# A fused mixer and gated-experts kernel: the first block's norm alone ahead of the first product, and the work of steps 0 to 3 in another order

## The reference

```python
xn = _layernorm(x)                         # mean and variance over the 128 channels
s = _L0_attn_ref(xn, ...)                  # token mixer: 6 projections, a scan over time, group norm, output projection
# experts, R = 4 rounds, E = 4 experts, top 2:
for r in range(R):
    logits = flat @ Wg[r] + bg[r]
    vals, idx = top_k(logits, 2); w = softmax(vals)
    cw = sum(one_hot(idx, E) * w[..., None], axis=1)
    hmid = gelu(einsum('nh,ehf->enf', flat, W1) + b1)
    y = einsum('enf,efh->enh', hmid, W2) + b2
    cur = cur + einsum('ne,enh->nh', cw, y)
out = x + s * silu(cur)
```

## Time and profile before

| | us |
|---|---|
| median of 3 runs | 797.25 (796.95 to 797.36) |
| the profiled execution | 795.54 |
| its span in the trace | 793.7 |
| PE busy | 781.5 (98% of the span) |
| DVE busy | 687.8 (87%) |
| ACT busy | 642.4 (81%) |
| POOL busy | 111.9 (14%) |

### The profile page before, as it was taken

The page is one execution under the profiler, slowest core; times in us unless marked ns, Lnnn a source line. Parts: engine busy times, 40 slices in busy tenths (PEclk is TensorE's granted clock), DMA queues, the critical chain, the costliest instruction groups (busy, mean ns, idle before and its releaser), DMA issues.

```text
span 793.7 us, 9921 instructions
## 1 busy us (share of the span) xinstructions
PE 781.5 (98%) x3395; PEld 620.5 (78%) x3395; DVE 687.8 (87%) x1090; ACT 642.4 (81%) x878; POOL 111.9 (14%) x135
## 2 busy tenths in 40 slices
PE   8899999999999999999999999999999999999996
PEld 6678788887888878888788887888878887788885
DVE  7988887899888889879899788987988989998997
ACT  7989887887888878788778877887878888788884
POOL 0011111111111101111111111111111111111110
PEclk9999999999999999999999999999999999999998
DMA  8444362342534326234164322643228544365452
GB/s 263 126 88 136 60 183 62 93 102 46 125 64 106 94 40 160 58 81 103 28 146 114 76 65 40 147 107 94 44 38 172 107 75 102 63 174 123 76 121 53
DMA packets 63569, 78.46 MB, mean 99 GB/s; under 512 B 36000, under 2 KB 41632, under 8 KB 59552
## 3 DMA queue, kind: packets, MB, share of 16 engines
q0 software_dynamic: 18144, 33.04, 24.7%
q1 hardware_dynamic: 45104, 44.67, 18.7%
q10 hardware_dynamic: 272, 0.13, 0.1%
HBM read 40.34 MB, written 2.36 MB: 54 GB/s over the span
## 4 chain that ended last, share of the span: by engine, by line
PE 91%; DVE 5%; ACT 1%; issue 1%; DMA 1%; DVEq 0%; ACTq 0%
PE h_bank L985 14%; PE h_bank L981 14%; PE h_bank L982 14%; PE y_bank L1045 14%; PE y_bank L1041 14%; PE y_bank L1040 14%; PE p_bank L981 2%; PE p_bank L985 2%; PE p_bank L982 2%; PE r_bank L1080 1%; DVE g_lo L690 1%; ACT g L408 1%; DVE tmp L704 1%; ACT g_hi L414 1%; DMA cw_b<-cw_scratch 0%
## 5 line engine op out<-in xcount | busy, mean ns | idle before, releaser
L408 ACT ACTIVATE g<-h_bank,b_c 128x512 f32<-128x512 f32 x512 | 329.3, 681 | 81.2 <-PE h_bank L985 80.6
L690 DVE TENSOR_TENSOR g_lo<-g,g_hi 128x1024 fp32r<-128x1024 f32 x256 | 310.3, 1222 | 83.5 <-ACT g_hi L414 81.9
L414 ACT ACTIVATE g_hi<-g 128x1024 fp32r<-128x1024 f32 x256 | 271.8, 1062 | 8.1
L356 POOL DMA_DIRECT2D cur<-tmp x126 | 110.8, 879 | 667.8 <-DVE tmp L704 516.9
L985 PE MATMUL h_bank<-cur_lo,w_hi 128*128 128x512 f32 x512 | 204.0, 398 | 0.0
L981 PE MATMUL h_bank<-cur_hi,w_hi 128*128 128x512 f32 x512 | 203.2, 397 | 0.2 <-DVE cur_hi L601 0.2
L1040 PE MATMUL y_bank<-g_hi,w_hi 128*128 128x512 f32 x508 | 200.7, 395 | 2.3 <-DVE w_lo L580 2.1
L982 PE MATMUL h_bank<-cur_hi,w_lo 128*128 128x512 f32 x512 | 202.6, 396 | 0.0
L1041 PE MATMUL y_bank<-g_hi,w_lo 128*128 128x512 f32 x508 | 200.7, 395 | 0.0
L1045 PE MATMUL y_bank<-g_lo,w_hi 128*128 128x512 f32 x508 | 139.6, 396 | 0.0
L981 PEld LDWEIGHTS h_bank<-cur_hi,w_hi 128*128 128x128 f32 x512 | 96.4, 188 | 27.6 <-issue 4.6
(11 more groups left out here) (144 smaller groups left out, 393.9 us busy)
## 6 DMA issues: line engine op xcount, KB each, us to landing
cur<-tmp POOLq DMA_DIRECT2D x126, 256.0 KB, 3.3
cw_b<-cw_scratch SPq DMA_DIRECT2D x31, 1024.0 KB, 5.0
cur<-in_x SPq DMA_DIRECT2D x8, 256.0 KB, 5.4
xn_t<-cur SPq DMA_DIRECT2D x8, 256.0 KB, 3.4
xr<-in_x SPq DMA_DIRECT2D x28, 64.0 KB, 3.4
out<-o SPq DMA_DIRECT2D x28, 64.0 KB, 2.0
cw_b<-in_w SPq DMA_DIRECT2D x4, 256.0 KB, 3.9
cw_b<-cw_scratch SPq DMA_DIRECT2D x1, 768.0 KB, 5.4
```

The lines of the kernel that those rows point to most:

```text
L356: pool.dma_start(cur[:, block_of(s // E)], tmp[:, s % SUMS, :], accum_op=ALU.add).then_inc(summed, DMA)
L408: nc.scalar.activation(g[:, gb, ft * BLK:(ft + 1) * BLK], hb[ft][:, :], ACT.Gelu_apprx_tanh, bias=b1_c[:, e * FT + ft:e * FT + ft + 1]).th ...
L414: nc.scalar.activation(g_hi[:, gb, h], g[:, gb, h], ACT.Copy).then_inc(g_hi_done, 1)
L690: nc.vector.tensor_tensor(g_lo[:, gb, h], g[:, gb, h], as_f32(g_hi[:, gb, h]), ALU.subtract).then_inc(g_lo_done, 1)
```

## The change

Four things change, none of which alters what is computed.

1. **Block 0 alone.** `norm_first` becomes `norm_one(b)`, which makes statistics, mean and variance of one block. `norm_one(0)` and `norm_root((0,))` stand ahead of the first product, `norm_one(1)` and `norm_root((1,))` behind `low_w2(0)`. PE's chain has 11 transposes in place of 13. `turn_first` writes `p_bank` and `r_bank`, `store_first` reads them and comes later on DVE. ACT scales block 1 after `hidden(0)`, not before it, and PE turns it after `down(0)`, not before `up(1)`.
2. **The third down projection in the logits' bank.** `down(2)` writes `r_bank` and waits for `router_scores(0)` to have read the logits, not for `combine(0)`.
3. **The router of blocks 0 and 1 later.** `logits(0)` moves from behind `up(1)` to behind `up(2)`, `router_scores(0)` to the end of DVE's step 0, `router_tanh(0)` to step 1 on ACT, `router_gates(0)` to the start of DVE's step 1. `combine(0)` and `combine(1)` both stand at the end of DVE's step 1.
4. **Blocks 2 and 3.** `norm_stats((2,))` stands at the start of DVE's step 2, `norm_stats((3,))` and `norm_spread` between the two halves of `g_low_half` of step 2, and the root at the start of step 3.

The high and low parts of `w2` move too: `high_w2(2)` and `high_w2(3)` to the start of ACT's steps 1 and 2, `low_w2(2)` and `low_w2(3)` to the ends of DVE's steps 0 and 1.

The diff, cut to what moves work:

```diff
-ROOT_CHAIN = 13
+ROOT_CHAIN = 11
-NORM_GROUPS = [(0, 1), (2, 3), (4, 5, 6, 7)]
+NORM_GROUPS = [(0,), (1,), (2, 3), (4, 5, 6, 7)]
-LATE = (0, 8)
+LATE = (0, 1, 8)
+IN_R_BANK = 2
...
             high_w2(0)
-            scale_block(1)
             act.wait_ge(b1_loaded, DMA)
             hidden(0)
+            scale_block(1)
...
                 if s == 1:
                     high_w1(3)
+                    high_w2(2)
+                elif s == 2:
+                    high_w2(3)
...
                 def between():
-                    if s < E - 1:
-                        high_w2(s + 1)
+                    if s == 0:
+                        high_w2(1)
...
                 def late():
-                    if s == 0:
+                    if s == 1:
                         router_tanh(0)
...
-            norm_first()
-            norm_root((0, 1))
+            norm_one(0)
+            norm_root((0,))
...
             low_w2(0)
-            store_first()
+            norm_one(1)
+            norm_root((1,))
+            low_w1(2)
             dve.wait_ge(gate_loaded, DMA * GATEW)
             nc.vector.tensor_scalar(wg_p[:, :, 0:E], wg_c[:, :, :], 1.0, None, ALU.mult).then_inc(combined, 2)
+            g_low_half(0, 0)
+            g_low_half(0, 1)
+            store_first()
             store_second()
-            g_low_half(0, 0)
-            low_w1(2)
-            g_low_half(0, 1)
-            router_scores(0)
...
                 if s == 1:
-                    split_cur(1)
+                    router_gates(0)
                 elif s == 2:
-                    norm_root(NORM_GROUPS[1])
+                    norm_stats((2,))
                 elif s == 3:
-                    norm_stats(NORM_GROUPS[2][0:2])
+                    norm_root(NORM_GROUPS[2])
+                elif s == 4:
+                    norm_stats(NORM_GROUPS[3][0:2])
...
                     if half == 0:
-                        if s < E - 1:
-                            low_w2(s + 1)
                         if s == 0:
-                            router_gates(0)
-                        elif s == 1:
-                            dve.wait_ge(small_loaded, DMA * SMALL)
-                            combine(0)
+                            low_w2(1)
+                        elif s == 2:
+                            norm_stats((3,))
+                            norm_spread(NORM_GROUPS[2])
...
                 if s == 0:
                     low_w1(3)
+                    low_w2(2)
+                    router_scores(0)
                 elif s == 1:
-                    norm_stats(NORM_GROUPS[1])
-                    norm_spread(NORM_GROUPS[1])
+                    split_cur(1)
+                    low_w2(3)
+                    dve.wait_ge(small_loaded, DMA * SMALL)
+                    combine(0)
+                    combine(1)
...
-                pe.wait_ge(combined, s + 1)
-                if s == 0:
-                    pe.wait_ge(p_empty, 1)
+                y = yb[b]
+                if s == IN_R_BANK:
+                    y = rb
+                    pe.wait_ge(r_empty, 1)
+                else:
+                    pe.wait_ge(combined, s + 1)
...
             up(0)
-            turn_normed(1)
...
-                if s == 0:
+                if s == 1:
                     logits(0)
...
+                if s == 0:
+                    turn_normed(1)
                 for b in at_step(NORM_SCALE, s):
                     turn_normed(b)
```

More of the change, by code:

```diff
@@ L539, in norm_stats, with norm_one @@
                 link(last)
[L541 to L550, removed]
+            def norm_one(b):
+                h = tiles_of((b,))
+                norm_stats((b,))
+                for c in range(b * TPB, (b + 1) * TPB):
+                    last = nc.vector.bn_aggr(mv[:, c, :], stats[:, c, :])
+                link(last)
+                link(nc.vector.tensor_scalar(veps[:, h], mv[:, h, 1], LN_EPS, None, ALU.add))
+                nc.vector.tensor_scalar(mean[:, h], mv[:, h, 0], 1.0, None, ALU.mult)
             def norm_spread(blocks):
@@ L592, in first_half @@
                 h = slice(n * TPB // 2, (n + 1) * TPB // 2)
-                return yb[n][:, 0:HALF].rearrange("p (i t) -> p i t", t=TPB // 2), h
+                return (pb, rb)[n][:, 0:HALF].rearrange("p (i t) -> p i t", t=TPB // 2), h
             def split_first():
@@ L696, in combine @@
                 q = k % 2
+                y = rb if s == IN_R_BANK else yb[s % 2]
                 dve.wait_ge(down_done, s + 1)
@@ L703, in combine @@
                     dve.wait_ge(summed, DMA * (s - SUMS + 1))
-                nc.vector.scalar_tensor_tensor(out=tmp[:, s % SUMS, :], in0=yb[s % 2][:, :], scalar=b2_c[:, e:e + 1],
+                nc.vector.scalar_tensor_tensor(out=tmp[:, s % SUMS, :], in0=y[:, :], scalar=b2_c[:, e:e + 1],
                                                in1=cw_b[:, q, e * BLK:(e + 1) * BLK],
@@ L877, in _ @@
                 if s == 1:
-                    split_cur(1)
+                    router_gates(0)
                 elif s == 2:
-                    norm_root(NORM_GROUPS[1])
+                    norm_stats((2,))
                 elif s == 3:
-                    norm_stats(NORM_GROUPS[2][0:2])
+                    norm_root(NORM_GROUPS[2])
+                elif s == 4:
+                    norm_stats(NORM_GROUPS[3][0:2])
                 elif s == 5:
-                    norm_stats(NORM_GROUPS[2][2:4])
+                    norm_stats(NORM_GROUPS[3][2:4])
                 elif s == 6:
-                    norm_spread(NORM_GROUPS[2])
-                    norm_root(NORM_GROUPS[2])
+                    norm_spread(NORM_GROUPS[3])
+                    norm_root(NORM_GROUPS[3])
                 elif s == 7:
@@ L987, in turn_normed @@
             def turn_normed(b):
-                if b > 1:
-                    pe.wait_ge(p_empty, b)
+                pe.wait_ge(p_empty, b)
                 pe.wait_ge(xn_ready, b + 1)
@@ L1003, in turn_first @@
                         pe.wait_ge(xn_ready, 1)
-                    ins = nc.tensor.transpose(yb[t // half][:, t % half:HALF:half], xn_st[:, 0, t * D:(t + 1) * D], ident[:, :])
+                    ins = nc.tensor.transpose((pb, rb)[t // half][:, t % half:HALF:half], xn_st[:, 0, t * D:(t + 1) * D], ident[:, :])
                     if t == half - 1:
@@ L1039, in down @@
                     hi = g_hi[:, b, ft * BLK:(ft + 1) * BLK]
-                    nc.tensor.matmul(yb[b][:, :], w2_hi[:, e * FT + ft, :], hi, start=(ft == 0), stop=False)
-                    nc.tensor.matmul(yb[b][:, :], w2_lo[:, e * FT + ft, :], hi, start=False, stop=False)
+                    nc.tensor.matmul(y[:, :], w2_hi[:, e * FT + ft, :], hi, start=(ft == 0), stop=False)
+                    nc.tensor.matmul(y[:, :], w2_lo[:, e * FT + ft, :], hi, start=False, stop=False)
                 for ft in range(FT):
@@ L1044, in down @@
                         pe.wait_ge(g_lo_done, 2 * s + ft // 2 + 1)
-                    last = nc.tensor.matmul(yb[b][:, :], w2_hi[:, e * FT + ft, :], g_lo[:, b, ft * BLK:(ft + 1) * BLK],
+                    last = nc.tensor.matmul(y[:, :], w2_hi[:, e * FT + ft, :], g_lo[:, b, ft * BLK:(ft + 1) * BLK],
                                             start=False, stop=(ft == FT - 1))
@@ L1106, in _ @@
             for _ in range(FILL):
-                nc.tensor.transpose(rb[:, 0:D], ident[:, :], ident[:, :])
+                nc.tensor.transpose(hb[FT - 1][:, 0:D], ident[:, :], ident[:, :])
             up(0)
-            turn_normed(1)
             for s in range(STEPS):
```

## The result

| | before | after |
|---|---|---|
| median, same chip, 6 runs each | 797.06 us (796.21 to 797.36) | 803.21 us (802.81 to 804.15) |
| ratio to before | | 1.0079 (95% interval 1.0068 to 1.0091) |
| the profiled execution | 795.54 | 803.53 |
| its span | 793.7 | 801.7 |

The change makes the kernel 6.15 us slower. 804.7 was predicted, in a range of 801.7 to 806.2.

A forecast was written before the change was run, and what follows sets the result against it. PE, busy for 98% of the span, was taken as the bound. Block 3's turning was to come 5.3 + 2.2 (waits, then half pace) = 7.5 later; 797.25 + 7.5 gave 804.7, range 801.7 to 806.2.

The forecast's parts named there:

- The start: First real transposes on PE: turn_first at 7.97 in place of 8.59, limited by PE's own queue, a gain of 0.62 us.
- Steps 0 to 2: PE up to down(3): wg_p at 15.7 costs 0.2, gates come at 28.35, PE wants down(3) at 34.2.
- Step 3: combine(1) at 35.55, root until 43.7; PE waits 2.1, 2.6 and 3.4; block 2 turned at 45.4, not 40.11.
- The clock: TensorE's granted clock falls in the 3.4 us wait for block 2; 4.4 us at half pace lose 2.2.
- Rival A: Clock falls in the wait for block 2: median 804.7, profiled execution 803.0; chance 0.57, the forecast.
- rival E: Clock falls twice, in the 2.6 us wait too or once more later: another 1 to 2, 806.5; chance 0.05.
- ACT's 0.4 of step 4: Before block 3's turning: ACT's scaling ends at 51.85, PE would be there at 51.45; hidden if the clock falls.
- B: Clock holds through the waits: 797.25 + 5.7 = 802.9; chance 0.28.
- C: Faster: gates come early enough and all three of PE's early losses go, 2.8 gained, 794.4; chance 0.06.
- D: No change: gates come 5.7 earlier than worked out, late norm just makes up the start's gain, 797.3; chance 0.04.

The follow-up runs named there:

- v1: Changed kernel with down(1) in p_bank, statistics of blocks 2 and 3 ahead of the combines, their root later, their scaling and turning one step later: 794.17 us.
- e_warm: Changed kernel with PE's three waits of steps 3 and 4 filled by identity transposes that nobody reads: 801.62 us, ratio to before 1.0068.
- e_norm_ahead: Changed kernel with statistics of blocks 2 and 3 and their combination ahead of combine(0), root at the start of step 2: 796.29 us, ratio to before 0.9996.
- e_no_gates: Changed kernel with combine(0) and combine(1) multiplying by loaded tokens instead of waiting for the gates (result wrong, for timing only): 800.49 us, ratio to before 1.0051.
- e_before_warm: Kernel before with 16 identity transposes ahead of down(3), so PE is not idle in its wait: 795.47 us, ratio to before 0.9982.
- e_turn_later: Changed kernel with scaling, turning and splits of blocks 2 and 3 one step later each: 798.25 us, ratio to before 1.0020.
- e_bank_only: Kernel before with only down(2) moved to the logits' bank: 796.99 us, ratio to before 0.9995.

## Why the prediction was right, and where its sizes were off

**The start** (0.62 expected, 0.34 at the first product). The step held: PE's queue and not DVE limits the start. DVE had the tiles at 6.85 + 0.60 and PE took them at 8.31, directly behind its chain. The end of the warm-up was taken from one profile, 6.76. It was 7.11 here, 7.37 in v1, 6.18 in e_warm and 6.01 in e_norm_ahead: the moment at which the pace of the transposes doubles moves from one execution to the next. So neither 0.62 nor 0.34 is the gain of the start; with the same start the first product came at 8.75 to 10.14, while the three profiles with the start of before have it at 9.97 to 10.39.

**Steps 0 to 2.** `wg_p` was expected at 15.7 and ended at 15.88, the gates at 28.35 and were ready at 28.70: 0.2 and 0.35 late, of which the start's shortfall of 0.28 explains most. PE was ready for `down(3)` at 34.8 and not at 34.2.

**Step 3.** `combine(1)` was expected at 35.55, started at 35.92; the root's end at 43.7, was 44.15. The waits were 2.0, 1.1 and 3.4 against 2.1, 2.6 and 3.4. The second is shorter not because `g_lo` came earlier but because PE came to it later: the clock had already fallen at 37.5, and the products ahead of the wait ran at half pace. In `e_no_gates`, where they ran at the full pace, that wait was 2.0. The loss is the same, in another row. The turning of block 2 came 5.9 later than before in place of 5.3, and the step behind it added 2.4 in place of 2.2, which is how 7.5 became 8.27.

**The clock.** Rival A was the forecast and it happened, but twice, as in rival E, whose price of another 1 to 2 it did not add: the first fall lies almost wholly in time in which PE would have waited (0.2 of it shows, by `e_warm`). I had taken the idle 2.07 of before as a length that leaves the clock alone. That was wrong as a reading: it was one execution. e_before_warm shows that the same wait lets the clock fall in half or more of them. A smaller misreading: a granted clock of 0.88 in the slice from 787 to 788 puts the fall three quarters of the way into the slice, where the prediction says a quarter; the 2.1 behind the last work is right. In e_warm and e_before_warm transposes that compute nothing kept the higher level, and with it 1.6 us. The rule that the prediction cited from the Trainium skill ("TensorE: Matmul & The Clock Gate", Part 1), that the lower level is the default and activity releases the array from it, agrees with the two returns: at 41.0 behind the products from 36.77 on, and at about 51.2 behind those from 45.97 on. The start takes a caution that the prediction lacks: the column of the granted clock reads 1.00 there from 0 on, and only the number of transposes in a us tells the slow pace (before):

```profile
4.00:5.00 1.00, 1.00 (x6) 1.00 1.09 381
...
7.00:8.00 1.00, 1.00 (x12) 1.00 1.15 319
```

**The term that was mis-sized.** The sum in the profiled execution was 795.54 + 7.5 = 803.0, and the profiled execution of the changed kernel took 803.53. The median came out at 803.21 and not at 804.7, because I added the same 7.5 to the median of before, 797.25. That median already contained a fall of the clock, worth 1.7; the one profile did not. The clock's part of the difference, which I had as 2.2 less ACT's 0.4 of step 4, is about 2 against an execution without a fall, and almost nothing against one with it.

**The rivals.** B (clock holds) gave 802.9, closer to the median than the 804.7 of A, but for a reason that did not occur: its profile would have shown the higher level throughout. So the median alone would have picked the wrong rival; the profile picks A. C and D needed the root before 37 or the gates 5.7 earlier; neither was near.

Not settled: how much of the remaining difference between `e_norm_ahead` and before is the start's gain and how much DVE's fuller queue takes back. By the medians they cancel within 0.1%. In the two profiles the first product comes 1.2 earlier (8.75 for 9.97) and block 3 is turned 0.4 later (46.56 for 46.16), so 1.6 is lost between the two; but the start moves from one execution to the next, and these are one each.

## What to carry to other kernels

Work that is moved "out of the way" in an in-order queue goes behind whatever waits there: before moving it behind an instruction that waits for a DMA, compare when that DMA lands with when the work's reader asks, and put it ahead if the queue would idle anyway. If the reader can be served one step later, moving the reader is the cheaper cure (two lines of a table gave 5 of the 6 us here). And before a profile is used as the base of a sum, look whether the runs of that kernel fall in groups, and in which of them the profile lies.

## What the runs showed of the hardware

- A wait of PE of about 2 us in the middle of dense work let the granted clock fall in some executions and not in others. In the kept traces it fell behind waits of 1.96 (the changed kernel) and 2.28 (`e_turn_later`) and held through waits of 2.07 (before), 2.13 (`e_norm_ahead`) and 2.29 (`e_bank_only`). In the kernel before 20 of 27 runs lie in a group 1.7 us above the other 7, and filling this one wait with transposes of the identity put all 11 runs into the lower group.
- The clock need not fall inside the wait. Behind the wait of 1.96, which ended at 36.77, it fell at about 37.5, while PE was busy again; behind the wait of 2.28, which ended at 37.17, at about 37.7.
- The moment at which the pace of the first transposes doubles differs between executions by over a us: the row behind the 26 starts between 6.01 and 7.37 in the kept traces.
